# A vision tower's first performer: the loop over images in a new order

## The chip, the cores and the metric

One core of one Trainium2 chip runs the whole program. The metric is the device time of one execution in microseconds (us). The kernel before took 2234.66 us, the median of three runs (2223.88 to 2236.14).

## The reference, cut to what matters

The program computes a tower of five parts on 32 images of 3x128x128. The change lies in the first part alone, the first performer, which the reference writes as follows (`t` is 1024 patches of 147 numbers per image; EMB is 64, M is 32):

```python
t = _unfold(x, 7, 4, 2)                      # 32 images, 1024 tokens, 147 numbers
h = _ln(x, n1g, n1b)
k, q, v = split(h @ kqvw + kqvb)             # 64 each
kp, qp = _prm_exp(k, wrand), _prm_exp(q, wrand)   # exp(x @ w.T - |x|^2/2), 32 features
D = einsum('btm,bm->bt', qp, sum(kp, 1))
kptv = einsum('btd,btm->bdm', v, kp)
y = einsum('btm,bdm->btd', qp, kptv) / D
y = v + (y @ projw + projb)
y + (gelu(_ln(y) @ w1 + b1) @ w2 + b2)
```

After it come a second performer, a projection, two attentions, a mixture of experts, a state-space layer and a gated mixture of experts. They are not touched.

## The kernel before, in words

`patches` works image by image. An image is eight tiles of 128 tokens. The patches are read from a row-ordered copy of the image into one of two buffers `X`; a layer norm's mean is folded into the weights, so only the inverse root is multiplied in.

Every engine runs its own function `body(t, p)`, one call per step `t`; `schedule` writes the first steps out, then a hardware loop of two steps, then the last steps. Nothing plans the order: it is the order of the lines in each `body`, and semaphores hold the engines together. One step moves up to five images along:

- SyncE: copies image t+1 into row order, loads image t, stores image t-4.
- VectorE: `exponent` (squared norms and z) of the second half of image t-2, `finish` of t-4 (the last sum, L1159), `attend` of t-3 (denominators, their reciprocal, y, v added at L1141, statistics of y), `aggregate2`, `statistics` and `aggregate` of image t (L1108, L1112), `normalise2` (L1153), `exponent` of the first half of t-1, `keep_kp` (L1128), a copy of the projected keys and values.
- GpSimd: the inverse roots (L1078 adds epsilon, L1080 is the power), the scaled patches `R` (L1091) and `H` (L1093), and `yb` = y + b2 (L1098).
- ScalarE: copies out of PSUM, squares (L1208), exponentials and Gelu. Exp and Gelu each load a table first.
- TensorE (L1300 to L1355): transposes of image t-1 (`turn_tail` L1246, `turn_main` L1258), the product with the weights, first the 21 remaining rows in slots of 32 rows (`matmul_tails`, L1272), then the 126 main ones (`matmuls`, L1283); keys times values of t-2 (L1312), the turned queries (L1318), the projection KP (L1326), the turned y of t-3 (L1334), first layer (L1343), numerators (L1296), second layer (L1354).

The product with the weights is cut in pieces of 4, 2, 1 and 1 tiles, with the other products set between them. The numerators are eight products, each of 32 rows by 65 columns, in two groups of four with `matmuls` between them; `KPs` holds the same keys and values four times over the partitions, and each product takes one slot of 32 rows of it.

The second performer, in `performer`, already takes its numerators in another way: `BD` holds KP in four copies side by side, a mask leaves of each copy only its own slot of rows (L507), and one product of 128 rows by 260 columns (L732) gives four tiles.

Of the kernel before, what the change touches and what calls it, by code (L numbers as in the profile page):

```python
# [13 lines left out]
PARTS = 128  # L14
# [731 lines left out]
def patches(nc, name, image, rows_c, dst, w):  # L746
# [11 lines left out]
    with ExitStack() as ctx:  # L758
# [13 lines left out]
        names = ("x_in0", "x_in1", "out0", "out1", "border", "stat", "aggr", "eps1", "rstd1", "norm", "trans", "tback", "rem", "kq", "sq", "v", "xd", "z", "exp",  # L772
                 "kv", "kvs", "qt", "rq", "kp", "kps", "num", "den", "rden", "ymul", "y", "yb", "stat2", "aggr2",
                 "eps2", "rstd2", "norm2", "yt", "yts", "m1", "gelu", "m2", "fin", "ones", "zero", "tail", "load", "gate", "edge", "tails", "copied0", "copied1")
# [208 lines left out]
        KPs = st.sbuf("KPs", [PARTS, EMB + 1])  # L983
# [23 lines left out]
        def every_other(t, b):  # L1007

            return t.rearrange("p (c b) e -> p b c e", b=2)[:, b]

# [11 lines left out]
        def schedule(eng, body, end=steps):  # L1022

            for t in range(6):
                body(t, t % 2)
            with eng.Fori(6, end, 2) as t:
                body(t, 0)
                body(t + 1, 1)
            for t in range(end, steps + 4):
                body(t, t % 2)  # L1030

# [3 lines left out]
        def _(sp):  # L1035
# [16 lines left out]
            def body(t, p):  # L1052
                if live(t + 1) and not (isinstance(t, int) and t < EARLY - 1):
                    copy(sp, t + 1, 1 - p)
                if live(t) and not (isinstance(t, int) and t < EARLY):
                    load(sp, t, p)
                if isinstance(t, int) and t == 1:
                    border()
                if live(t - 4):
                    store(t - 4, p)  # L1060

            schedule(sp, body, steps - 2)
# [5 lines left out]
        def _(pool):  # L1068
# [5 lines left out]
            nc.gpsimd.memset(BDz[:], 0.0).then_inc(s["zero"], 1)  # L1074

# [6 lines left out]
            def body(t, p):  # L1082
                l = t - 3
                if live(l):
                    inverse_root(l, "aggr2", "eps2", "rstd2", mv2, rstd2)
                if live(t):
# [3 lines left out]
                    wait(pool, s["trans"], 3 * t)  # L1090
                    nc.gpsimd.tensor_tensor(R[:, :, 1:1 + REM].rearrange("p t (a b) -> p t a b", b=7), windows(p, 18, 3),  # L1091
                                            spread(spread(rstd[:], 2, 3), 3, 7), ALU.mult).then_inc(s["tail"], 1)
                    nc.gpsimd.tensor_tensor(H[:].rearrange("p t (a b) -> p t a b", b=7), windows(p, 0, 18),  # L1093
                                            spread(spread(rstd[:], 2, 18), 3, 7), ALU.mult).then_inc(s["norm"], 1)
                if live(l):
                    pool.wait_ge(s["y"], l + 1)
# [3 lines left out]
            schedule(pool, body)  # L1100

        @block.vector
        def _(dve):
            def statistics(i, p):
                wait(dve, s["eps1"], i)
# [4 lines left out]
            def aggregate(i):  # L1110
                for j in range(tiles):
                    nc.vector.bn_aggr(mv[:, j, :], stats[:, j, :]).then_inc(s["aggr"], 1)  # L1112

            def exponent(i, q):

                tl = slice(4 * q, 4 * q + 4)
                dve.wait_ge(s["sq"], quads * i + q + 1)
                nc.vector.reduce_sum(xd[:, tl, :], sq[:, tl, :, :], axis=AX_X).then_inc(s["xd"], 1)  # L1118
                dve.wait_ge(s["xd"], quads * i + q + 1)
                wait(dve, s["exp"], i)  # L1120
                dve.wait_ge(s["v"], quads * i + q + 1)
                nc.vector.tensor_tensor(z[:, :, tl, :].rearrange("p a t f -> p t a f"), KQ[q][:, :, 3 * EMB:COLS].rearrange("p t (a f) -> p t a f", a=2),
                                        spread(xd[:, tl, :], 3, FEATS), ALU.subtract).then_inc(s["z"], 1)

            def keep_kp(i):
                dve.wait_ge(s["kp"], i + 1)
                wait(dve, s["num"], 2 * i)
                nc.vector.tensor_copy(KPs[:], KP).then_inc(s["kps"], 1)  # L1128

            def attend(i, p):  # L1130
# [6 lines left out]
                wait(dve, s["yb"], i)  # L1137
                for b in range(2):
                    nc.vector.tensor_tensor(every_other(y[:], b), NUM[b][:, :, 0:EMB], spread(rden[:, b, :], 2, EMB), ALU.mult).then_inc(s["ymul"], 1)
# [6 lines left out]
            def aggregate2(i):  # L1146
                for j in range(tiles):
# [14 lines left out]
            def body(t, p):  # L1162
                l = t - 3
                if live(t - 2):
                    exponent(t - 2, quads - 1)
                if live(t - 4):
                    finish(t - 4, p)
                if live(l):
                    attend(l, 1 - p)


                    dve.wait_ge(s["stat2"], tiles * (l + 1))
                    dve.sem_inc(s["gate"], 1)
                    aggregate2(l)
                if live(t):
                    statistics(t, p)
                    dve.wait_ge(s["stat"], tiles * (t + 1))
                    dve.sem_inc(s["gate"], 1)
                    aggregate(t)
                if live(l):  # L1180
                    normalise2(l)
                if live(t - 1):
                    exponent(t - 1, 0)
                if live(t - 2):
                    keep_kp(t - 2)

            schedule(dve, body)

        @block.scalar
        def _(act):  # L1190
            def body(t, p):
                m, k, l = t - 1, t - 2, t - 3
                if live(m):
                    act.wait_ge(s["trans"], 3 * m + 1)
                    nc.scalar.copy(RQ[:, 0:256], bank(3)[:, 0:256]).then_inc(s["rem"], 1)
                    for q in range(quads):
                        act.wait_ge(s["trans"], 3 * m + 2 + q)
                        nc.scalar.copy(hT[0:MAIN, q, :], ps[0:MAIN, q * BANK:(q + 1) * BANK]).then_inc(s["tback"], 1)
                if live(k):
                    act.wait_ge(s["z"], quads * (k + 1))  # L1200
                    wait(act, s["qt"], k)
                    nc.scalar.activation(kpq[:].rearrange("p a t f -> p (a t f)"), z[:].rearrange("p a t f -> p (a t f)"), ACT.Exp).then_inc(s["exp"], 1)

                def squares(q):
                    tl = slice(4 * q, 4 * q + 4)
                    act.wait_ge(s["kq"], quads * m + q + 1)
                    wait(act, s["xd"], quads * m)
                    nc.scalar.activation(sq[:, tl, :, :].rearrange("p t a e -> p t (a e)"), KQ[q][:, :, 0:2 * EMB], ACT.Square,  # L1208
                                         scale=0.5 ** 0.5).then_inc(s["sq"], 1)

                    wait(act, s["y"], m - 1)
                    if isinstance(m, int) and m == 0:
                        act.wait_ge(s["ones"], 3)
                    nc.scalar.copy(v1[1 - p][:, tl, 0:EMB], KQ[q][:, :, 2 * EMB:3 * EMB]).then_inc(s["v"], 1)

                if live(m):
                    squares(0)
                if live(k):
                    act.wait_ge(s["kv"], k + 1)
                    nc.scalar.copy(kvT[:], spread(KV, 1, 4)).then_inc(s["kvs"], 1)  # L1220
                if live(k):
                    act.wait_ge(s["qt"], k + 1)
                    nc.scalar.copy(RQ[:, 256:256 + PARTS * quads], bank(7)[:, 256:256 + PARTS * quads]).then_inc(s["rq"], 1)
                if live(l):
                    act.wait_ge(s["yt"], l + 1)
                    nc.scalar.copy(yT[:].rearrange("p t c -> p (t c)"), bank(7, half)).then_inc(s["yts"], 1)
                if live(l):
                    act.wait_ge(s["m1"], l + 1)
# [1723 lines left out]
```

## Time and profile before

| | |
|---|---|
| Median of the runs | 2234.66 us (2223.88 to 2236.14) |
| Profiled execution | 2229.52 us, span 2227.8 us |
| TensorE busy | 1716.7 us, 77% |
| VectorE, ScalarE, GpSimd busy | 1092.0, 751.6, 734.2 us |
| Mean granted TensorE clock | 0.875 of 2.4 GHz |
| The first performer's loop | from about 31.4 us to about 530 us of the span |

Busy times are sums over one profiled execution. A matmul's end is modelled, and the next may begin before it; therefore the times of TensorE are best read from start to start. An fp32 product stands in the trace as two records or more.

### The profile page before, as it was taken

To read this page: it belongs to the slowest core of one execution; us is meant where nothing else is said; L and a number is where in the kernel's file an instruction comes from. 1 tells how busy PE (TensorE), PEld (TensorE's weight loads), DVE (VectorE), ACT (ScalarE), POOL (GpSimd) and SP (SyncE) were. 2 spreads that over 40 slices of the span, in tenths; PEclk is the share of its full clock that TensorE was granted. 3 is DMA by queue.
4 is the path that set the end of the run, shared out by engine and by line. 5 is a ranking of instruction groups with operands and counts; after the bars stand their busy time and mean duration, and the time that the engine had idled before them with its cause. 6 is when DMAs were issued, how large, how long until landed. Compare 5 with 4: busy or idle time off the path is not lost. (4 is left out here: it accounts for less than half of the span.)

```text
span 2227.8 us, 35707 instructions
## 1 busy us (share of the span) xinstructions
PE 1716.7 (77%) x11543; PEld 1310.8 (59%) x11544; DVE 1092.0 (49%) x3245; ACT 751.6 (34%) x1396; POOL 734.2 (33%) x664
## 2 busy tenths in 40 slices
PE   4898888983799956497768777999639767746897
PEld 3666666651688846376637676999627523335565
DVE  3666566562577631427653753122170179962232
ACT  1555555550255521125213623211114623213110
POOL 2545555441122210043141310333220069940232
PEclk9999999995899978698877966999859989976899
DMA  3222232211333313200000044555230176636111
GB/s 67 53 51 59 55 59 56 53 36 36 97 83 91 89 27 85 60 1 2 12 1 1 2 124 124 163 154 155 76 69 1 31 183 160 159 76 169 41 48 30
DMA packets 219403, 157.95 MB, mean 71 GB/s; under 512 B 116583, under 2 KB 196404, under 8 KB 218794
## 3 DMA queue, kind: packets, MB, share of 16 engines
q1 hardware_dynamic: 203141, 138.82, 25.6%
q0 software_dynamic: 6528, 14.19, 2.2%
q10 hardware_dynamic: 9638, 3.69, 0.7%
q8 instruction: 57, 0.93, 0.2%
q14 instruction: 39, 0.32, 0.1%
HBM read 106.05 MB, written 32.35 MB: 62 GB/s over the span
## 5 line engine op out<-in xcount | busy, mean ns | idle before, releaser
L2180 POOL TENSOR_TENSOR ssm_scan_prod<-ssm_scan_S,ssm_crep 128x1056 f32<-128x1056 f32 x48 | 159.4, 3321 | 157.9 <-DVE ssm_scan_S L2197 157.9
L677 PE MATMUL a_psum<-a_W,a_hT 128*128 128x256 f32 (+1 forms) x640 | 149.9, 382 | 12.5 <-ACT a_hT L586 12.5
L1283 PE MATMUL a_psum<-a_W,a_hT 126*128 126x256 f32 x512 | 144.8, 406 | 0.0
L677 PEld LDWEIGHTS a_psum<-a_W,a_hT 128*128 128x128 f32 (+1 forms) x640 | 118.5, 191 | 30.6 <-ACT a_hT L586 16.4
L2221 PE MATMUL ssm_scan_psum<-ssm_ST,ssm_EW 112*128 112x512 f32 (+1 forms) x288 | 103.6, 497 | 23.3 <-PEq L1935 20.5
L2735 PE MATMUL moe_tiles_psum<-moe_tiles_XT,moe_tiles_mine 96*128 96x128 f32 x960 | 118.7, 280 | 1.9 <-DMA moe_tiles_mine<-moe_W 1.9
L1118 DVE TENSOR_REDUCE a_xd<-a_sq 128x8 f32<-128x512 f32 x64 | 43.9, 685 | 149.5 <-ACT a_sq L1208 149.5
L2735 PEld LDWEIGHTS moe_tiles_psum<-moe_tiles_XT,moe_tiles_mine 96*128 96x128 f32 x960 | 113.0, 194 | 4.9 <-DMA moe_tiles_mine<-moe_W 2.3
L2197 DVE TENSOR_TENSOR_SCAN ssm_scan_S<-ssm_scan_X,ssm_scan_psum 128x1056 f32<-128x1056 f32 x48 | 112.9, 2353 | 5.1 <-issue 0.9
L1283 PEld LDWEIGHTS a_psum<-a_W,a_hT 126*128 126x128 f32 x512 | 89.2, 194 | 32.1 <-issue 18.9
L1080 POOL TENSOR_TENSOR a_rstd<-a_rstd,a_mhalf 128x8 f32<-128x8 f32 x64 | 105.1, 1642 | 5.0
L2221 PEld LDWEIGHTS ssm_scan_psum<-ssm_ST,ssm_EW 112*128 112x128 f32 x288 | 51.4, 192 | 90.0 <-issue 68.0
L1078 POOL TENSOR_TENSOR a_rstd<-a_mv,a_eps 128x8 f32<-128x8 f32 x64 | 22.9, 358 | 235.0 <-DVE a_mv L1148 209.5
L2782 ACT ACTIVATE moe_tiles_GT<-moe_tiles_psum 128x512 f32<-128x512 f32 x80 | 39.1, 490 | 160.5 <-PE moe_tiles_psum L2735 160.4
L2827 DVE TENSOR_TENSOR moe_tiles_Y<-moe_tiles_psum,moe_B 128x192 f32<-128x192 f32 x40 | 14.3, 357 | 156.8 <-PE moe_tiles_psum L2719 156.8
L2209 ACT ACTIVATE ssm_scan_psum<-ssm_scan_psum 128x1056 f32<-128x1056 f32 x48 | 49.7, 1035 | 120.4 <-PE ssm_scan_psum L2221 120.4
L2762 PE MATMUL glu_tiles_psum<-glu_W,glu_tiles_XT 96*128 x192 | 84.6, 585 | 6.3 <-DVE glu_tiles_XT L2812 6.1
L2719 PE MATMUL moe_tiles_psum<-moe_W,moe_tiles_GT 128*128 x480 | 84.5, 326 | 0.0
L2078 PE MATMUL ssm_mlp_psum<-ssm_mlp_xT,ssm_mlp_W 96*128 96x260 f32 (+3 forms) x352 | 82.0, 393 | 0.6 <-ACT ssm_mlp_xT L1903 0.6
L1208 ACT ACTIVATE a_sq<-a_psum 128x512 f32<-128x512 f32 x64 | 38.2, 597 | 129.7 <-PE a_psum L1283 129.7
L2690 POOL DMA_INDIRECT ys<-moe_tiles_Y,moe_target x40 | 39.5, 987 | 128.6 <-DVE moe_tiles_Y L2827 125.7
L2719 PEld LDWEIGHTS moe_tiles_psum<-moe_W,moe_tiles_GT 128*128 128x128 f32 x480 | 77.1, 190 | 0.0
(633 smaller groups left out, 3986.5 us busy)
## 6 DMA issues: line engine op xcount, KB each, us to landing
ssm_scan_grep<-gains SPq DMA_DIRECT2D x48, 528.0 KB, 4.7
moe_tiles_mine<-moe_W SPq DMA_DIRECT2D x40, 576.0 KB, 3.9
a_X<-t SPq DMA_DIRECT2D x168, 96.0 KB
moe_route_raw<-in_L_ffn_w SPq DMA_DIRECT2D x16, 576.0 KB
t<-a_O SPq DMA_DIRECT2D x128, 64.0 KB
xrows<-in_x SPq DMA_DIRECT2D x30, 192.0 KB
a_X<-xrows SPq DMA_DIRECT2D x60, 91.9 KB
proj_X<-t SPq DMA_DIRECT2D x96, 48.0 KB
```

The lines of the kernel that those rows point to most:

```text
L677: last = nc.tensor.matmul(out, hT[0:rows, kt, cols], W[0:rows, kt, :], start=(kt == 0), stop=(kt == nkt - 1))
L1080: nc.gpsimd.tensor_tensor(out[:], out[:], mhalf[:], ALU.pow).then_inc(s[done], 1)
L1118: nc.vector.reduce_sum(xd[:, tl, :], sq[:, tl, :, :], axis=AX_X).then_inc(s["xd"], 1)
L1283: last = nc.tensor.matmul(KQ[q][:, j, :], hT[0:MAIN, q, PARTS * j:PARTS * j + PARTS], W[0:MAIN, :], start=False, stop=True)
L2078: last = nc.tensor.matmul(ps[0:rows_, (n % 4) * BANK:(n % 4) * BANK + GROUP], W1[0:k, kb, c0:c0 + rows_], xT[0:k, kb, GROUP * g:GROUP * g ...
L2180: nc.gpsimd.tensor_tensor(prod[n % 2][:], S[n % 2][:], crep[:, cols], ALU.mult).then_inc(s_prod, 1)
L2197: nc.vector.tensor_tensor_scan(S[n % 2][:], X[n % 2][:], E[n % 2], 0.0, ALU.add, ALU.mult).then_inc(s_scan, 1)
L2209: nc.scalar.activation(E[n % 2], E[n % 2], ACT.Exp).then_inc(s_coef, 1)
L2221: last = nc.tensor.matmul(E[n % 2][:, a:b], EW[:, j, :], ST[:, j // (NCH // 2), HCOLS * h + a:HCOLS * h + b], start=True, stop=True)
L2719: last = nc.tensor.matmul(made(p), GT[p][0:w_, f, :], W2[0:w_, f, bass.ds(e, 1), :].rearrange("p a c -> p (a c)"), start=(f == 0), stop=(f ...
L2735: last = nc.tensor.matmul(hidT(1 - p, f, 1), mine[q][0:HALF + kb, kb, PARTS * f:PARTS * f + PARTS], XT[1 - p][0:HALF + kb, kb, :], start=( ...
L2762: last = nc.tensor.matmul(hid(c), XT[p][0:k, kb, :], W1[0:k, kb, bass.ds(e, 1), cut * c:cut * c + cut].rearrange("p a c -> p (a c)"), star ...
```

## The change

The mathematics stays. What changes in the first performer's loop:

- VectorE's order is now: finish image t-6; block diagonal of t-4; aggregate t-1; exponent second half of t-3; attend and aggregate2 of t-4; statistics of t; normalise2 of t-4; exponent first half of t-2. The aggregation of an image's statistics is a step later than the statistics.
- GpSimd does the first inverse root, R and H ahead of the second inverse root and yb (of t-3).
- ScalarE, TensorE and SyncE get the orders shown below; up to seven images are under way, and the store is of image t-7. The loops of `schedule` have a lag of their own per engine and more steps written out.
- The eight numerators become two products of 128 rows by 260 columns. `KPs` becomes `BD`, made with a mask by one VectorE operation. The halves of y are now contiguous. The mask is built at the start on GpSimd, behind the zeroing of the border (L1074), and VectorE's first operation waits for it.
- Several counters are split by half (kq0, kq1 and so on), and waits are added where buffers are reused across steps.

```diff
+            dve.wait_ge(s["ones"], 7)
...
-                nc.vector.tensor_copy(KPs[:], KP).then_inc(s["kps"], 1)
+                nc.vector.tensor_tensor(BD[:], spread(KP, 1, 4), spread(mask[:], 2, EMB + 1), ALU.mult).then_inc(s["kps"], 1)
...
@@ vector, body
+                if live(t - 6):
+                    finish(t - 6, p)
                 if live(t - 4):
+                    keep_kp(t - 4)
+                if live(t - 1):
+                    aggregate(t - 1)
+                if live(t - 3):
+                    exponent(t - 3, 1)
+                if live(t - 4):
+                    attend(t - 4, p)
+                    aggregate2(t - 4)
                 if live(t):
                     statistics(t, p)
+                if live(t - 4):
+                    normalise2(t - 4)
                 if live(t - 2):
+                    exponent(t - 2, 0)
...
@@ scalar, body (m, k, l, n = t - 1, t - 2, t - 3, t - 4)
+  gelu(n); values(m, 0); squares(m, 0); kvT(k); RQ queries(k); squares(m, 1); values(m, 1);
+  yT(l); hT halves 0, 1 of image t; RQ remainder of t; exp(m)
...
@@ tensor
+            def numerators(i):
+                pe.wait_ge(s["kps"], i + 1)
+                pe.wait_ge(s["rq"], i + 1)
+                wait(pe, s["yts"], i)
+                for q in range(quads):
+                    nc.tensor.matmul(NUM[q].rearrange("p t c -> p (t c)"), RQ[:, 256 + PARTS * q:256 + PARTS * q + PARTS], BD[:].rearrange("p r c -> p (r c)"),
+                                     start=True, stop=True).then_inc(s["num"], 1)
...
             def body(t, p):
+                if live(t - 5):
+                    mlp2(t - 5)
+                if live(t - 4):
+                    turn_y(t - 4)
+                if live(t - 3):
+                    project_keys(t - 3)
+                if live(t - 1):
+                    turn_tail(t - 1)
+                    turn_main(t - 1, 1)
+                if live(t - 3):
+                    numerators(t - 3)
+                if live(t - 4):
+                    mlp1(t - 4)
+                if live(t - 1):
+                    first_half(t - 1)
+                if live(t - 2):
+                    keys_values(t - 2, p)
+                if live(t - 1):
+                    second_half(t - 1)
+                if live(t):
+                    turn_main(t, 0)
+                if live(t - 2):
+                    turn_queries(t - 2)
+                if live(t - 1):
+                    last_mains(t - 1)
```

The two lines under "scalar, body" stand for the new order of that engine's operations, whose own code is unchanged but for its waits. `first_half` and `second_half` hold four remainder products each, and the eight main ones are cut 4, 2 and 2; `mlp1`, `mlp2`, `turn_y`, `project_keys`, `keys_values` and `turn_queries` are the products of before under names of their own.

## Rows read from the trace of the kernel before

**Rows 1.** Page, part 1: busy time, share, instructions.

```profile
PE 1716.7 (77%) x11543; PEld 1310.8 (59%) x11544; DVE 1092.0 (49%) x3245; ACT 751.6 (34%) x1396; POOL 734.2 (33%) x664
```

**Rows 2.** Windows, first to 29th finish, then the drain: length, busy, granted clock, DMA.

```profile
72.45:483.64 411.19, 364.64 (x2578) 251.38 (x2577) 264.54 (x1262) 228.40 (x392) 213.92 (x196) 0.95 0.28 55
483.64:529.99 46.35, 26.86 (x156) 17.59 (x154) 21.02 (x80) 14.52 (x23) 9.23 (x9) 0.69 0.07 18
```

**Rows 3.** Timeline of TensorE, one step: start, duration, line, operation, records, idle before.

```profile
263.64 0.38 PE L1246 MATMUL a_psum<-a_ident,a_R 128*128 128x128 f32 x2
...
269.82 1.13 PE L1283 MATMUL a_psum<-a_W,a_hT 126*128 126x256 f32 x4
272.06 0.44 PE L1326 MATMUL a_psum<-a_projw,a_kvT 65*128 65x65 f32 x2 [1.10 <-ACT a_kvT L1220]
...
272.88 0.60 PE L1283 MATMUL a_psum<-a_W,a_hT 126*128 126x256 f32 x2
273.80 1.12 PE L1343 MATMUL a_psum<-a_yT,a_w 128*128 128x512 f32 x2 [0.32 <-ACT a_yT L1226]
274.86 0.66 PE L1296 MATMUL a_psum<-a_KPs,a_RQ 32*128 32x65 f32 x8
275.44 0.70 PE L1283 MATMUL a_psum<-a_W,a_hT 126*128 126x256 f32 x2
276.07 0.66 PE L1296 MATMUL a_psum<-a_KPs,a_RQ 32*128 32x65 f32 x8
276.67 1.16 PE L1354 MATMUL a_psum<-a_w,a_G 128*128 128x128 f32 x8
277.66 0.38 PE L1246 MATMUL a_psum<-a_ident,a_R 128*128 128x128 f32 x2
278.72 0.55 PE L1258 MATMUL a_psum<-a_ident,a_H 128*126 128x128 f32 x3 [0.24 <-DVE a_O L1159]
```

**Rows 4.** Timeline of TensorE in the second performer: its block-diagonal numerators.

```profile
684.53 0.60 PE L732 MATMUL a_psum<-a_BD,a_RQ 128*128 128x260 f32 x2
684.97 0.61 PE L739 MATMUL a_psum<-a_w,a_G 128*128 128x128 f32 x4
```

**Rows 5.** Windows: a stretch with the clock down, and the second performer.

```profile
139.00:140.00 1.00, 1.00 (x2) 0.00 (x0) 0.00 (x0) 0.88 (x1) 1.00 (x1) 0.55 0.09 12
149.00:150.00 1.00, 1.00 (x4) 0.92 (x5) 0.84 (x10) 0.99 (x2) 0.00 (x0) 0.83 0.27 66
660.00:720.00 60.00, 56.74 (x344) 50.17 (x345) 43.08 (x157) 32.27 (x59) 17.49 (x28) 1.00 0.33 90
```

**Rows 6.** Timeline of VectorE: two finishes, one step apart, and the wait between.

```profile
249.75 0.69 DVE L1159 TENSOR_TENSOR a_O<-a_psum,a_yb 128x512 f32<-128x512 f32 x1
...
254.19 1.76 DVE L1108 BATCH_NORM_STATS2 a_stats<-a_X 128x6 f32<-128x147 f32 x8
...
262.79 0.69 DVE L1118 TENSOR_REDUCE a_xd<-a_sq 128x8 f32<-128x512 f32 x1 [3.91 <-ACT a_sq L1208]
...
263.85 0.68 DVE L1159 TENSOR_TENSOR a_O<-a_psum,a_yb 128x512 f32<-128x512 f32 x1
```

**Rows 7.** Timelines of GpSimd and VectorE where they meet.

```profile
256.83 0.56 POOL L1078 TENSOR_TENSOR a_rstd<-a_mv,a_eps 128x8 f32<-128x8 f32 x1 [0.55 <-DVE a_mv L1112]
...
259.69 1.95 POOL L1093 TENSOR_TENSOR a_H<-a_X,a_rstd 128x1008 f32<-128x1008 f32 x1
...
490.12 1.26 POOL L1098 TENSOR_TENSOR a_yb<-a_y,a_b 128x512 f32<-128x512 f32 x1
490.19 1.75 DVE L1153 TENSOR_TENSOR a_yn<-a_y,a_rstd 128x512 f32<-128x512 f32 x1 [2.04 <-POOL a_rstd L1080]
```

**Rows 8.** Timelines at the loop's start, and an affine select of later.

```profile
31.43 1.80 DVE L1108 BATCH_NORM_STATS2 a_stats<-a_X 128x6 f32<-128x147 f32 x8 [0.32 <-PEq L798]
...
31.88 1.85 POOL L1074 MEMSET a_BDz<- 32x2112 f32 x1
...
534.85 0.29 POOL L60 TENSOR_SCALAR_AFFINE_SELECT a_ident<-a_ident 128x128 f32<-128x128 f32 x1 [0.16 <-POOL a_ident L58]
```

More of the change, by code:

```diff
@@ L1020, in live, with schedule, upto @@
             return 0 <= i < steps if isinstance(i, int) else True
[L1022 to L1024 removed]
+        def schedule(eng, body, lag, end=steps):
+            first = lag + 2 + lag % 2
+            for t in range(first):
                 body(t, t % 2)
[L1026 removed]
+            with eng.Fori(first, end, 2) as t:
                 body(t, 0)
                 body(t + 1, 1)
[L1029 removed]
+            for t in range(end, steps + lag):
                 body(t, t % 2)
+        def upto(n):
+            return min(n, steps) if isinstance(n, int) else n
         block = ctx.enter_context(nc.Block())
@@ L1182, in body @@
-                if live(t - 1):
-                    exponent(t - 1, 0)
+                if live(t - 4):
+                    normalise2(t - 4)
                 if live(t - 2):
-                    keep_kp(t - 2)
-            schedule(dve, body)
+                    exponent(t - 2, 0)
+            schedule(dve, body, 6)
         @block.scalar
         def _(act):
-            def body(t, p):
-                m, k, l = t - 1, t - 2, t - 3
-                if live(m):
[L1194 to L1217, printed above, removed]
@@ new lines, in squares, with values @@
+            def squares(i, q):
+                tl = slice(4 * q, 4 * q + 4)
+                act.wait_ge(s["kq%d" % q], i + 1)
+                wait(act, s["xd%d" % q], i)
+                nc.scalar.activation(sq[:, tl, :, :].rearrange("p t a e -> p t (a e)"), KQ[q][:, :, 0:2 * EMB], ACT.Square,
+                                     scale=0.5 ** 0.5).then_inc(s["sq%d" % q], 1)
+            def values(i, q, p):
+                tl = slice(4 * q, 4 * q + 4)
+                act.wait_ge(s["kq%d" % q], i + 1)
+                wait(act, s["y"], i - 1)
+                if isinstance(i, int) and i == 0:
+                    act.wait_ge(s["ones"], 3)
+                nc.scalar.copy(v1[p][:, tl, 0:EMB], KQ[q][:, :, 2 * EMB:3 * EMB]).then_inc(s["v%d" % q], 1)
@@ L1218, in body @@
+            def body(t, p):
+                m, k, l, n = t - 1, t - 2, t - 3, t - 4
+                if live(n):
+                    act.wait_ge(s["m1"], n + 1)
+                    wait(act, s["m2"], n)
+                    nc.scalar.activation(G[:].rearrange("p t c -> p (t c)"), bank(0, half), ACT.Gelu, bias=b1[:, 0:1]).then_inc(s["gelu"], 1)
+                if live(m):
+                    values(m, 0, 1 - p)
+                    squares(m, 0)
                 if live(k):
                     act.wait_ge(s["kv"], k + 1)
+                    wait(act, s["kp"], k)
@@ new lines, in turn_y, with mlp1 @@
+            def turn_y(i):
+                pe.wait_ge(s["norm2"], i + 1)
+                pe.wait_ge(s["rq"], upto(i + 2))
+                for j in range(tiles // 2):
+                    last = nc.tensor.transpose(bank(7)[:, PARTS * j:PARTS * j + PARTS],
+                                               yn[:, 2 * j:2 * j + 2, :].rearrange("p t e -> p (t e)"), ident[:])
+                last.then_inc(s["yt"], 1)
+            def mlp1(i):
+                pe.wait_ge(s["yts"], i + 1)
+                pe.wait_ge(s["th0"], upto(i + 4))
+                if isinstance(i, int):
+                    wait(pe, s["gelu"], i)
+                nc.tensor.matmul(bank(0, half), w1[:], yT[:].rearrange("p t c -> p (t c)"), start=True, stop=True).then_inc(s["m1"], 1)
```

245 lines of the change are left out of this document (107 added, 138 removed), and 3 rows, old and new, of the table names.

## The prediction

> **What bounds the kernel now.** I read the page's busy times first [rows 1]: TensorE is busy 77% of the span, but that is a mean over five parts with different limits, so the loop has to be read alone. The windows do that [rows 2]: between the first and the 29th finish lie 411.19 us, 28 steps, 14.69 us each, and in them TensorE is busy 364.6 (89%), VectorE 264.5, ScalarE 228.4, GpSimd 213.9. Per step that is 9.45 us of VectorE, 8.16 of ScalarE, 7.64 of GpSimd: TensorE is the nearest to its limit, the others have 4.6 us or more to spare. VectorE even stands still 3.91 us in the middle of a step, until the squares that wait for the last main product [rows 6].
>
> Then one step of TensorE, from start to start [rows 3]: turn_tail begins at 263.64 and 277.66, 14.02 us apart (finish to finish 14.10 [rows 6]). In it TensorE waits for others: from the end of the second cut's two main products (269.82 + 1.13 = 270.95) to KP at 272.06, 1.11 us for ScalarE's copy kvT; before the first layer 0.32 us for yT; 0.24 us for the finish in a part of the steps. A following group that doesn't wait begins some 0.1 to 0.15 before the modelled end of the one ahead (277.66 against 276.67 + 1.16 = 277.83), so a wait costs that more than its idle time.
>
> Last the clock. 28 steps of 14.10 make 394.8; the window is 16.4 longer. The granted clock of the window is 0.95 [rows 2]: about 41 us of it lie at half clock (1.2 instead of 2.4 GHz). One such stretch runs from 139.1 to 149.3 by its two edges [rows 5], 10.2 us, so there are four, at 4.1 us each. The rows don't say what starts a fall; I take TensorE's idle time as the cause.
>
> **The change part by part.** All for one steady step, at full clock.
>
> 1. The waits. kvT of image t-3 is now copied by ScalarE a step ahead of the product that reads it; its cost of 1.11 + 0.13 goes. turn_y comes at the step's start and the first layer some 2.0 us after it, with turn_tail, turn_main and the numerators between; today turn_y and the copy of its result to yT together take less than 1.74 (KP at 272.06, first layer at 273.80), so they fit. 0.32 + 0.1 go. The finish is awaited by turn_main only three images on: 0.24 in one step of two, about 0.2 with its overlap. Exponentials are made half a step ahead of keys times values: some 0.2. Sum 2.0; only the bare idle of the rows is 1.11 + 0.32 + 0.12 = 1.55, the lower bound.
> 2. Numerators. Two groups of four take 275.44 - 274.86 = 0.58 and 276.67 - 276.07 = 0.60 [rows 3]. The product of 128 rows by 260 columns in the second performer takes 684.97 - 684.53 = 0.44 [rows 4]; two make 0.88. Gain 0.3, and from 0.1 (0.15 more for loading the first weights after another kind of product) to 0.35.
> 3. Main products cut 4, 2, 2 instead of 4, 2, 1, 1: the two single ones take 273.48 - 272.88 = 0.60 and 276.07 - 275.44 = 0.63; a pair 1.13 less 0.13 = 1.0. Gain 0.2, from 0 to 0.25.
> 4. VectorE gets 128x260 with a mask for a 128x65 copy. The trace has no product of this kind in this loop, but one of 128x256 from PSUM beside a small operand in z; by 0.42 against 0.22, +0.2 us, off the path as long as VectorE has room. It stands between KP and the numerators, though, with turn_tail and turn_main as cover (0.7 us).
> 5. The start. The mask comes behind the memset of the border (31.88 + 1.85 = 33.73), a memset and two selects of 0.29 each with a handoff of 0.16 [rows 8]: VectorE's first statistics begin at 34.6 instead of 31.43. **+3.2 us**, bounds +2.5 and +4.
> 6. SyncE stores t-7 and no longer waits for a fresh finish in front of the next copy and load. VectorE never waited for a load. Nothing gained; the load still waits for H of t-2 and has about 6 us before the statistics.
>
> 14.02 - 2.0 - 0.3 - 0.2 = 11.5 us per step if TensorE is never idle. By the lower bounds 14.02 - 1.55 - 0.1 = 12.4; by the upper 11.3. I take **11.7**, near the full sum, because the waits are read directly and the rest is small.
>
> **Do the other engines follow at 11.7?** I laid them out from the start of the second layer at 0: it ends at 1.16, finish to 1.8, KP done at 1.9, block diagonal to 2.4 (the numerators begin at 2.5), aggregate to 2.8, exponent to 3.9, attend and aggregate2 to 7.75, statistics to 9.45. GpSimd: aggregate done 2.9, yb of the image before ends 3.2, inverse root 5.3, R and H to 8.2, second inverse root 10.2. VectorE normalises at 10.2, then exponent to 11.9. turn_y wants the first at 12.7 and turn_tail the second at 13.5: about 1.5 us to spare. ScalarE: yT 1.7, hT and remainder to 3.6, z there at 4.0, table and exponentials to 5.9, table and Gelu to 7.8 (needed at 11.7), then it waits for the first main products. The ring through VectorE and GpSimd closes at about 10.6, so TensorE stays the bound, but narrowly.
>
> **Sum.** 28 steps of 11.7 are 327.6 against 411.2: -83.6, of which 16.4 is the clock, which I expect to stay up: the second performer with TensorE busy 56.74 of 60 us has 1.00 [rows 5]. First finish: an image lies 4 steps less 254.19 - 249.75 = 4.4 us, 52.0, between statistics and finish today, and takes 72.45 - 31.43 = 41.0 while the loop fills, 0.79 of it. Now it is 6 steps less about 6.5: 63.7, times 0.79 is 50: **+9** (0 to +12). Drain: from the 29th finish to the end are 46.35 us, two whole rounds through attend, inverse root, Gelu and finish one behind the other, at clock 0.69 [rows 2]. In the new order attend of the last image stands ahead of the finish of the image before, so one round is left: three intervals of about 10, 10 and 8: **-17.7** (-8 to -24). With the start +3.2: -83.6 - 17.7 + 9 + 3.2 = -89.1. From the profiled execution's 2229.5 this gives 2140.4; the median of the runs shown is 5.1 above the profiled time, so I say **2142**.
>
> **A rule that speaks against part 2.** Four products of 32 rows by 65 columns take 0.58 here, where 260 columns at full height take 0.44 [rows 3, 4]. The Trainium skill (TensorE: Matmul & The Clock Gate, Part 3, Measured speedup vs the span model) says that small row tiles run at the same time, the span being that of one product plus some ns per tile; by that alone two rounds of 65 columns would be some 0.22 us (an estimate, twice a quarter of 0.44), and the change would lose 0.66 a step instead of gaining 0.3. The rows don't agree: 1.18 against 0.88 is measured, and decides.
>
> **Rivals.**
> A, VectorE and GpSimd bound. An operation with two SBUF inputs is stopped by GpSimd: yn took 1.75 instead of 0.66 while yb ran, and the epsilon add 0.56 instead of 0.20 beside yn [rows 7]. Today they are set apart. In the new order y + v (two SBUF inputs, at 5.2) falls on R and H (5.3 to 8.2), and yn on yb (10.2). If GpSimd is first both times, VectorE loses 1.95 + 1.1 = 3.05, 1.5 more than there is to spare: 13.3 us a step, 28 x 13.3 = 372.4, in all 2229.5 - 38.8 - 5.5 = **2185**. The Trainium skill (SBUF — State Buffer, Who interferes with whom) has this rule, the whole instruction being blocked, as rows 7 show. Against it: by my layout y + v comes 0.1 ahead of R, so R waits, not it.
> B, the clock still falls. The new order puts turn_y, KP, turn_tail and turn_main in a row, 1.5 us without a wide product. At today's one fall of 10.2 us per 103 us (411.19/4) there are 3.2 in 328 us, each now costing its whole half, 5.1 us: +16, **2158**.
> C, the loop is held as before: ScalarE's order (table load behind its wait, Gelu behind exponentials) or the new reuse waits keep TensorE at 14 us. 28 x 14.1 + 16.4 is what it was, and with 9 + 3.2 - 17.7 the time is **2224**. Against: 3.9 us between Gelu and its use.
> D, slower. The stretch of part B, once every step, keeps the clock down for much of the loop. A share f at half clock makes the step 11.7/(1 - f/2): the loop breaks even with 14.69 at f = 0.41. At f = 0.55, 16.1 us: 28 x 16.1 = 451, +40, with fill and drain about +8: **2277** at worst. Against: in the loop today the same transposes beside idle time bring it down only one step in six.
>
> **Chances.** Forecast 0.60; B 0.17; A 0.12; C 0.06; D 0.05. The measurement tells 0.5% (11 us) from no change: faster 0.89, same 0.06, slower 0.05. With 11.3 per step and the better drain it would be 2122; the range goes from there to A, 2187. C and D are left out, and what is under the forecast's lower end.
>
> **What would show it.** Finish to finish 11.4 to 12.0 us; no idle of TensorE before KP and the first layer; granted clock 1.00 through the loop; L732's kind of record (380 ns) for the numerators; block diagonal about 0.43; first statistics at 34.6; last finish near 440 instead of 530; everything behind it unchanged. y + v above 0.7 or yn at 1.75 speaks for A, clock 0.95 for B, idle TensorE with a steady 14 for C. I am wrong if the step is above 12.4 at full clock.

## The result, and the profile after

The kernel after takes **2116.99 us** (median of four runs, 2113.64 to 2117.62) against 2231.6 for the kernel before in the same runs: ratio 0.950, interval 0.947 to 0.952. I had said 2142, with 2122 to 2187 as the range: the direction and the case (TensorE the bound, full clock) were right, the gain was larger than I said, and the time lies 5 us below the range.

The profiled execution has a span of 2111.6 us against 2227.8. Part 1 of its page, columns as in [rows 1]:

```profile
PE 1653.1 (78%) x11159; PEld 1297.2 (61%) x11160; DVE 1096.1 (52%) x3245; ACT 744.2 (35%) x1394; POOL 732.7 (35%) x667
```

TensorE is busy for 64 us less. VectorE, ScalarE and GpSimd are busy as long as before (1096, 744 and 733 us), in a shorter span. The windows that answer to [rows 2] do, first to 29th finish and 29th finish to the end of the loop:

```profile
84.86:389.53 304.67, 302.13 (x2238) 237.55 (x2237) 264.89 (x1237) 222.78 (x392) 206.94 (x192) 1.00 0.34 70
389.53:417.10 27.57, 18.32 (x72) 12.03 (x70) 13.01 (x55) 7.50 (x12) 7.49 (x7) 0.62 0.11 29
```

TensorE is busy 302.1 of 304.7 us (it was 364.6 of 411.2), at a granted clock of 1.00. The parts, against the forecast:

| | before | after | change | forecast |
|---|---|---|---|---|
| first finish | 72.45 | 84.86 | +12.4 | +12.2 (+3.2 start, +9 fill) |
| 28 steps | 411.19 | 304.67 | -106.5 | -83.6 |
| drain | 46.35 | 27.57 | -18.8 | -17.7 |
| span behind the loop | | | -3.3 | 0 |
| sum | | | -116.2 | -89.1 |

First finish and drain came out within 1.1 us. The code behind the loop is the same in both kernels; no row here shows a cause for its -3.3 us, and the profiled execution after is itself 3.35 us below the median of its runs, so I take it as scatter. Of the miss of 27.1 us, 22.9 are in the step: 10.88 us on the mean (10.85 and 10.96 in turn) where I took 11.7.

One step of TensorE after, from one second-layer product to just ahead of the next (279.94), and below the second dots one row of the next step; columns as in [rows 3]:

```profile
269.10 1.06 PE L1358 MATMUL a_psum<-a_w,a_G 128*128 128x128 f32 x8
269.99 0.60 PE L1341 MATMUL a_psum<-a_ident,a_yn 128*128 128x128 f32 x4
270.43 0.33 PE L1327 MATMUL a_psum<-a_projw,a_kvT 65*128 65x65 f32 x2
270.60 0.39 PE L1268 MATMUL a_psum<-a_ident,a_R 128*128 128x128 f32 x2
271.03 0.63 PE L1279 MATMUL a_psum<-a_ident,a_H 128*126 128x128 f32 x4
271.49 1.04 PE L1334 MATMUL a_psum<-a_BD,a_RQ 128*128 128x260 f32 x4
272.37 1.02 PE L1350 MATMUL a_psum<-a_yT,a_w 128*128 128x512 f32 x2
273.32 0.71 PE L1284 MATMUL a_psum<-a_Wrem,a_RQ 32*128 32x256 f32 x8
...
277.45 1.13 PE L1290 MATMUL a_psum<-a_W,a_hT 126*128 126x256 f32 x4
278.42 0.60 PE L1279 MATMUL a_psum<-a_ident,a_H 128*126 128x128 f32 x4
278.86 0.38 PE L1321 MATMUL a_psum<-a_ident,a_kpq 128*128 128x128 f32 x2
279.08 1.03 PE L1290 MATMUL a_psum<-a_W,a_hT 126*128 126x256 f32 x4
...
281.99 0.63 PE L1279 MATMUL a_psum<-a_ident,a_H 128*126 128x128 f32 x4 [0.15 <-DVE a_O L1179]
```

In this step no record shows idle time ahead of it. Only turn_tail (270.60) to turn_main (271.03) is 0.43 instead of 0.22, since turn_main waits for the finish; in every other step that wait shows as 0.15 us of idle time (281.99). Read from start to start as in the prediction, this is where the step's 3.2 us went:

| stretch, start to start | before | after | less |
|---|---|---|---|
| two main products, wait for kvT | 2.24 | 0.97 | 1.27 |
| third and fourth main product, wait for yT | 1.55 | 0.86 | 0.69 |
| numerators | 1.18 | 0.88 | 0.30 |
| turn_tail and both halves of turn_main, wait for the finish | 1.54 | 1.33 | 0.21 |
| KP and turn_y | 0.82 | 0.61 | 0.21 |
| turned queries | 0.35 | 0.22 | 0.13 |
| first layer | 1.06 | 0.95 | 0.11 |
| second layer | 0.99 | 0.89 | 0.10 |
| four main products (with a wait), keys times values, remainders | 4.29 | 4.13 | 0.16 |

The four rows ahead of the last one are products that the change only moved. I had given them nothing.

VectorE in the same step:

```profile
268.00 0.69 DVE L1173 TENSOR_TENSOR a_yn<-a_y,a_rstd 128x512 f32<-128x512 f32 x1 [0.50 <-POOL a_rstd L1089]
...
270.19 0.69 DVE L1179 TENSOR_TENSOR a_O<-a_psum,a_yb 128x512 f32<-128x512 f32 x1 [0.37 <-PE a_psum L1358]
270.80 0.43 DVE L1144 TENSOR_TENSOR a_BD<-a_psum,a_mask 128x260 f32<-128x260 f32 x1
...
271.69 0.65 DVE L1134 TENSOR_REDUCE a_xd<-a_sq 128x8 f32<-128x512 f32 x1
...
274.00 0.69 DVE L1158 TENSOR_TENSOR a_y<-a_y,a_v 128x512 f32<-128x512 f32 x1
```

and GpSimd:

```profile
274.26 0.77 POOL L1098 TENSOR_TENSOR a_R<-a_X,a_rstd 128x168 f32<-128x168 f32 x1
```

The block diagonal takes 0.43. y + v at 274.00 comes 0.26 ahead of R at 274.26, takes its plain 0.69, and R is stretched from 0.48 to 0.77; yn takes 0.69, not the 1.75 of [rows 7] (once, while the loop fills, at 71.69, it took 1.74). VectorE stands still 0.50 and 0.37 us in the two waits shown.

At the start the mask costs what was said:

```profile
34.61 1.80 DVE L1121 BATCH_NORM_STATS2 a_stats<-a_X 128x6 f32<-128x147 f32 x8 [3.22 <-POOL a_mask L1082]
...
46.73 1.38 DVE L1121 BATCH_NORM_STATS2 a_stats<-a_X 128x6 f32<-128x147 f32 x6 [6.88 <-DMA a_X<-xrows]
```

The second line is one that I did not foresee: the third image's load lands only at 46.7, and VectorE waits 6.88 us for it. (The row is cut at the end of its window; the wait ahead of it is whole.)

### The profile page after: what moved, and what is told of

Read it like the earlier page. It is cut to its first block and busy times, and to the rows that moved or that the text cites. A ratio compares the mean times of both kernels' runs of the same rounds, so it can differ in the third digit from the quotient of the medians.

```text
span 2111.6 us, 35070 instructions
## 1 busy us (share of the span) xinstructions
PE 1653.1 (78%) x11159; PEld 1297.2 (61%) x11160; DVE 1096.1 (52%) x3245; ACT 744.2 (35%) x1394; POOL 732.7 (35%) x667
## 5 line engine op out<-in xcount | busy, mean ns | idle before, releaser
L677 PEld LDWEIGHTS a_psum<-a_W,a_hT 128*128 128x128 f32 (+1 forms) x640 | 118.5, 191 | 30.7 <-ACT a_hT L586 16.4
L1290 PE MATMUL a_psum<-a_W,a_hT 126*128 126x256 f32 x512 | 134.7, 396 | 0.0
L2109 PEld LDWEIGHTS ssm_mlp_psum<-ssm_mlp_xT,ssm_mlp_W 96*128 96x128 f32 (+3 forms) x352 | 66.7, 190 | 14.3 <-ACT ssm_mlp_xT L1934 0.9
L1109 POOL TENSOR_TENSOR a_yb<-a_y,a_b 128x512 f32<-128x512 f32 x32 | 40.7, 1272 | 93.0 <-DVE a_O L1179 93.0
L2265 PE MATMUL ssm_scan_psum<-ssm_scan_prod,ssm_SEL 128*32 128x264 f32 x384 | 32.3, 409 | 45.5 <-POOL ssm_scan_prod L2211 45.5
```

Source lines behind the costliest of these rows:

```text
L677: last = nc.tensor.matmul(out, hT[0:rows, kt, cols], W[0:rows, kt, :], start=(kt == 0), stop=(kt == nkt - 1))
L1290: last = nc.tensor.matmul(KQ[q][:, j, :], hT[0:MAIN, q, PARTS * j:PARTS * j + PARTS], W[0:MAIN, :], start=False, stop=True)
L2109: last = nc.tensor.matmul(ps[0:rows_, (n % 4) * BANK:(n % 4) * BANK + GROUP], W1[0:k, kb, c0:c0 + rows_], xT[0:k, kb, GROUP * g:GROUP * g ...
```

## The experiments

The question was where the missing 0.8 us a step comes from, whether idle time was the cause of the clock's falls, and how near the other engines are. Theory L, formed from the table above: a group of products whose first weight load cannot run ahead of the stream, because it stands behind a wait or beside products of 32 rows, costs about 0.1 us more, and in a dense stream that goes. Its rival O: a group costs what its own records say, only the idle time in the rows is to be had. "Step" is finish to finish, mean of 28 in one profiled execution. The diffs are shortened, and some of their lines are in words.

**1. The new numerators alone, in the old order.**

```diff
 kernel before
-                nc.vector.tensor_copy(KPs[:], KP).then_inc(s["kps"], 1)
+                nc.vector.tensor_tensor(BD[:], spread(KP, 1, 4), spread(mask[:], 2, EMB + 1), ALU.mult)...
-                for j in (0, 1, 4, 5) if first else (2, 3, 6, 7): ...32-row products
+                one 128 x 260 product for each half
```

> The kernel before in its old order with the numerators as two block-diagonal products (and the mask at the start, +3 us). Theory O: 0.44 for each in place of 0.58 and 0.60, the step falls by 0.3 to 13.7 us, 2231 - 8 + 3 = 2226. Theory L: the groups behind the 32-row ones (main product, second layer) also get their weight loads covered, the step falls by 0.5 to 13.5, 2231 - 14 + 3 = 2220. The clock's falls stay under both.

Measured: 2207.39 us (2201.32 to 2210.32), ratio 0.989 (0.986 to 0.992); step 13.78. TensorE's timeline of it:

```profile
264.38 1.12 PE L1349 MATMUL a_psum<-a_yT,a_w 128*128 128x512 f32 x2 [0.32 <-ACT a_yT L1236]
265.33 0.60 PE L1303 MATMUL a_psum<-a_BD,a_RQ 128*128 128x260 f32 x2
265.77 0.60 PE L1293 MATMUL a_psum<-a_W,a_hT 126*128 126x256 f32 x2
266.21 0.60 PE L1303 MATMUL a_psum<-a_BD,a_RQ 128*128 128x260 f32 x2
266.65 1.05 PE L1360 MATMUL a_psum<-a_w,a_G 128*128 128x128 f32 x8
267.54 0.38 PE L1256 MATMUL a_psum<-a_ident,a_R 128*128 128x128 f32 x2
...
268.83 0.66 PE L1268 MATMUL a_psum<-a_ident,a_H 128*126 128x128 f32 x4 [0.48 <-DVE a_O L1169]
```

From the first layer to turn_tail it is 3.16 us, against 277.66 - 273.80 = 3.86 in [rows 3]: 0.70 less, and only 0.30 of it is the numerators' own. The first layer went from 1.06 to 0.95, the second from 0.99 to 0.89, and the single main product between the numerators from 0.63 to 0.44. So the part of L that speaks of 32-row products holds for these. The part on waits does not hold for the first layer, which stands right behind a wait of 0.32 and takes 0.95 all the same. The experiment also takes the reason from part 3 of my prediction: a single main product among full-height ones costs 0.44, half of the pair's 0.86 to 0.87. Cutting costs nothing; the 32-row neighbours did. The step fell by less than 0.70, from 14.10 to 13.74 outside one fall of the clock, and the wait for the finish grew from 0.24 to 0.48. The time is 13 us under the lower expectation mainly because I had left the falls in: one step of 15.18 is all that is left of them.

**2. The kernel after with the old numerators.** The same edit, undone in the new order: the two groups of four stand one behind the other, and the second waits for the first.

> The changed kernel in its new order with the eight old numerators of 32 rows, the second four behind a wait for the first four. Theory O: step 10.88 + 0.3 = 11.2 us, and the start is 3 us earlier without the mask: 2117 + 9 - 3 = 2123. Theory L: the first layer behind them loses its early weight load too and the second group of four stands exposed: 11.4 to 11.5, 2117 + 16 - 3 = 2130.

2140.74 us (2130.64 to 2143.2), ratio 0.959; step 11.52, +0.64. Its timeline:

```profile
264.09 1.39 PE L1332 MATMUL a_psum<-a_KPs,a_RQ 32*128 32x65 f32 x16
265.41 1.12 PE L1349 MATMUL a_psum<-a_yT,a_w 128*128 128x512 f32 x2
266.47 0.71 PE L1278 MATMUL a_psum<-a_Wrem,a_RQ 32*128 32x256 f32 x8
```

The numerators take 1.32 (1.18 before, with another product between the groups) and the first layer behind them is back at 1.06: 0.55 of 0.64. The rest stands ahead of them, at turn_main, 0.56 instead of 0.46. The part of the 1.32 that is the wait of the second group is not separated. The clock stayed at 1.00 in the 28 steps. 28 steps at 0.64 are 18 of the 24 us between the two times, both above what I had expected. The first finish, at 89.58, is 4.7 later, though the statistics begin 3.1 earlier: while the loop filled, one y + v took 2.10 beside GpSimd, TensorE stood still 2.65 us (until 73.06), and its clock was 0.88, 0.50 and 0.60 in the three stretches of 5 us from 70 to 85 us.

**3. The wait for kvT alone, in the old order.** ScalarE copies kvT and the queries ahead of the first squares.

```diff
 kernel before, scalar body
-                if live(m):
-                    squares(0)
                 if live(k): ...copy kvT, copy RQ queries
+                if live(m):
+                    squares(0)
```

> The kernel before with one swap: ScalarE copies kvT and the turned queries ahead of the squares and values of the first half. It takes away TensorE's wait before KP (1.11 us of idle time a step) and nothing else; the waits for yT and the finish stay. Theory O (own times: a wait costs its idle time and the 0.13 us by which groups otherwise overlap, what I used in the prediction): the step falls from 14.02 to 12.8 us; KP keeps its 0.36 us to the next group's start. Theory L (a group behind a wait also pays for its first weight load, which in a dense stream runs ahead): KP falls to about 0.17, the step to 12.6. On the clock: if the idle time before KP starts the falls, they vanish and 28 steps save another 16 us: 2231 - 39 - 16 = 2176 (L) or 2181 (O); if they stay, 2192 to 2197.

2189.47 us (2186.63 to 2190.93), ratio 0.981 (0.979 to 0.984); step 13.28 and no fall of the clock in the loop. TensorE:

```profile
263.64 1.13 PE L1283 MATMUL a_psum<-a_W,a_hT 126*128 126x256 f32 x4
264.61 0.33 PE L1326 MATMUL a_psum<-a_projw,a_kvT 65*128 65x65 f32 x2
265.22 0.66 PE L1334 MATMUL a_psum<-a_ident,a_yn 128*128 128x128 f32 x4 [0.28 <-DVE a_yn L1153]
```

The wait of 1.11 is gone and the two main products take 0.97, as in the kernel after; KP's record is 0.33 instead of 0.44. But the step gave only 0.8 of 1.27, less than either theory said: a new wait of 0.28 for yn stands behind KP. A wait read from a row is worth its length only if no other engine's ring (a chain of work that closes on itself once a step) is as long.

**4. Both small edits in the old order.**

> The kernel before with both small edits: kvT copied ahead of the squares, and the numerators as two block-diagonal products. Apart they took the step from 14.10 to 13.30 and 13.74 us. If TensorE's order alone held the loop, the two would add up to 14.10 - 1.43 - 0.70 = 12.0 us (theory L's full price of each). Theory R, that the old order closes a ring (squares of the second half, exponent, finish, second half of turn_main), says that a part comes back as a longer wait for the finish, as in e_bd_only (0.48 us in place of 0.24): 12.8 us, 2231 - 36 - 16 + 3 = 2182.

2196.52 us (2191.57 to 2201.4), ratio 0.985; step 13.28, the same as with experiment 3 alone, where I had expected 12.8. (The time is longer than there because the first finish, behind the mask, is 5.1 later.) What the numerators save on TensorE comes back whole, in TensorE's wait for the finish, 0.26 in experiment 3:

```profile
276.53 0.66 PE L1268 MATMUL a_psum<-a_ident,a_H 128*126 128x128 f32 x4 [0.94 <-DVE a_O L1169]
```

and VectorE in the same stretch:

```profile
274.27 0.69 DVE L1128 TENSOR_REDUCE a_xd<-a_sq 128x8 f32<-128x512 f32 x1 [2.37 <-ACT a_sq L1218]
...
275.79 0.69 DVE L1169 TENSOR_TENSOR a_O<-a_psum,a_yb 128x512 f32<-128x512 f32 x1 [0.37 <-POOL a_yb L1106]
```

VectorE waits 2.37 us for the squares of the last main product, then makes the exponent, and only then the finish, for which the next image's turn_main waits. Last main product, squares, exponent, finish, turn_main: that ring of the old order closes at about 13.3 us in both experiments, though TensorE has some 0.7 less to do in the second. The new order opens it: VectorE's finish (270.19 in the kernel after) stands ahead of the exponent of the second half (271.69) instead of behind it. That this, more than any single wait, is what the new order is worth follows from the rows; no run changes VectorE's order alone.

**5. Idle time put back into the new order.** KP waits for ScalarE's first copy of hT.

```diff
 kernel after, tensor body
                 if live(t - 3):
+                    if live(t - 1):
+                        pe.wait_ge(s["th0"], t)
                     project_keys(t - 3)
```

> The changed kernel with one wait added: KP waits for ScalarE's first hT copy, which by the trace ends 1.28 us after KP's start, so TensorE stands still 1.3 us a step. Theory O: step 10.88 + 1.28 + 0.13 = 12.3 us, KP at 0.17 us to the next start. Theory L: KP goes back to 0.36 and the step to 12.5. Clock: if an idle stretch beside transposes starts the falls, the granted clock of the loop drops below 1.00 again, some four falls at 4 us each; if not, it stays 1.00. O without falls 2117 + 39 = 2156, L with falls 2117 + 45 + 16 = 2178.

2155.72 us (2152.7 to 2161.55), ratio 0.968; step 12.19, +1.31.

```profile
270.29 0.60 PE L1341 MATMUL a_psum<-a_ident,a_yn 128*128 128x128 f32 x4
272.06 0.44 PE L1327 MATMUL a_psum<-a_projw,a_kvT 65*128 65x65 f32 x2 [1.16 <-ACT a_hT L1247]
272.33 0.39 PE L1268 MATMUL a_psum<-a_ident,a_R 128*128 128x128 f32 x2
```

A bare idle of 1.16 costs 1.31 in all. In its own place it costs 1.33 (turn_y to KP is 1.77 instead of 0.44), KP is 0.27 instead of 0.17 to the next start and the numerators are 0.98 instead of 0.88; on the other side turn_tail is down from 0.43 to 0.23, since the finish is now there in time. And the clock stayed at 1.00 in all 28 steps, with as much idle time ahead of KP as the kernel before had (1.10), though without the waits for yT and the finish (0.32 and 0.24). This much idle time alone does not start the falls.

**6. Both put back: idle time and 32-row numerators in the new order.**

> The kernel after with both of two earlier edits: KP waits for the first copy of hT (about 1.16 us of idle TensorE a step) and the numerators are again eight products of 32 rows by 65 columns. Neither alone brought a clock fall. Theory both: idle time and the 32-row numerators together start the falls of the kernel before, so some steps of the 28 are 2 us or more longer and the granted clock of the loop is 0.95 to 0.98. Rival, order: the falls belong to the old order of the products, the clock stays at 1.00 and the step is the sum of the two edits, 10.88 + 1.31 + 0.64 = 12.8.

2194.30 us in one run; clock 0.92 in the loop, and eleven of the 28 steps are 14.2 to 16.0 us where the others take 12.55 to 12.8. So the falls came back, in the new order, with the two together. Here one begins:

```profile
127.80 0.43 PE L1321 MATMUL a_psum<-a_projw,a_kvT 65*128 65x65 f32 x2 [1.16 <-ACT a_hT L1241]
128.08 0.39 PE L1262 MATMUL a_psum<-a_ident,a_R 128*128 128x128 f32 x2
128.30 0.60 PE L1273 MATMUL a_psum<-a_ident,a_H 128*126 128x128 f32 x4
128.83 1.39 PE L1332 MATMUL a_psum<-a_KPs,a_RQ 32*128 32x65 f32 x16
130.15 1.84 PE L1349 MATMUL a_psum<-a_yT,a_w 128*128 128x512 f32 x2
```

Windows of it, columns as in [rows 2], before and after that point:

```profile
128.00:130.00 2.00, 1.93 (x24) 1.62 (x23) 1.66 (x11) 0.86 (x2) 1.01 (x3) 1.00 0.09 26
130.00:132.00 2.00, 2.00 (x10) 0.46 (x8) 1.84 (x7) 1.72 (x2) 1.92 (x3) 0.61 0.22 65
```

The clock goes from full (2.4 GHz) to half (1.2 GHz) inside the second window, whose mean is 0.61, behind idle time, transposes and 32-row numerators in a row; the first layer's record grows from 1.12 to 1.84. That stretch is what precedes the fall, but it is not the whole condition: the step before has the same stretch (KP at 115.13, behind 1.16 of idle time) and the clock stays at 1.00 there.

**7. VectorE's room: 8 more bn_stats a step.**

```diff
 kernel after, vector body, ahead of normalise2(t - 4)
+                    for j in range(tiles):
+                        nc.vector.bn_stats(junk[:, j, :], y[:, j, :])
```

> The changed kernel with eight more statistics of y per step on VectorE (1.11 us), written to a tile that nobody reads, between the statistics and normalise2. It measures how narrowly TensorE is the bound. VectorE stands idle 0.41 + 0.50 us a step. If VectorE has only that to spare, the step grows by about 0.2 us, to 11.1 (2123). If the added work meets the ring through GpSimd in full (rival A's mechanism), it grows by 0.6 or more, to 11.5 (2134). If TensorE has more room ahead than I think, nothing changes: 10.9.

2117.11 us (2115.47 to 2121.83), ratio 0.949; step 10.93, +0.05 for 1.1 us of work, less than the 0.2 that VectorE's waits would have made. TensorE stays the bound.

**8. The same with 24, 3.1 us.**

> The kernel after with 24 more bn_stats of 64 columns per step on VectorE, ahead of normalise2 (about 3.3 us; 8 of them, 1.1 us, made the step 0.05 longer). This is the loss of VectorE that rival A of the prediction supposed. Theory: VectorE becomes the bound and the ring through it has about 1.1 us to spare, so the step is 10.9 + 3.3 - 1.1 = 13.1 or a little more. Rival: VectorE has more room than its idle time shows, as its waits move too, and the step stays under 12.

2210.75 us in one run, loop clock 0.95. The undisturbed steps are 12.76 and 13.08, mean 12.9, so VectorE's ring has about 3.1 - 2.0 = 1.1 us to spare (I had expected 13.1). The other eleven take 15.2 to 15.6. TensorE in such a one:

```profile
275.84 0.66 PE L1345 MATMUL a_psum<-a_ident,a_yn 128*128 128x128 f32 x4 [1.03 <-DVE a_yn L1174]
...
276.99 0.41 PE L1272 MATMUL a_psum<-a_ident,a_R 128*128 128x128 f32 x2 [0.32 <-DVE a_z L1139]
277.92 0.91 PE L1283 MATMUL a_psum<-a_ident,a_H 128*126 128x128 f32 x4 [0.52 <-DVE a_O L1180]
278.62 1.94 PE L1338 MATMUL a_psum<-a_BD,a_RQ 128*128 128x260 f32 x4
```

GpSimd and then VectorE behind it:

```profile
281.58 1.95 POOL L1103 TENSOR_TENSOR a_H<-a_X,a_rstd 128x1008 f32<-128x1008 f32 x1
```

```profile
281.89 2.18 DVE L1159 TENSOR_TENSOR a_y<-a_y,a_v 128x512 f32<-128x512 f32 x1
```

1.87 us of idle time in three pieces, among transposes, and the numerators run at half clock: 1.94 instead of 1.04. So y + v comes behind R and H instead of ahead of them (0.31 behind H's start) and takes 2.18 instead of 0.69. Rival A's mechanism is real, and here it came by way of rival B's. The numerators are full-height ones, so 32-row numerators are not needed for a fall where there is more idle time than the 1.16 of experiment 5.

**9. A shorter path for the finish: second layer half a step earlier.** `mlp2(t - 4)` between turn_queries and last_mains instead of `mlp2(t - 5)` at the step's start.

> The changed kernel with the second layer of an image moved from the head of TensorE's step to the step before, between the turned queries and the last two main products. Its finish can then come 0.87 us earlier and turn_main's second half no longer waits for it. If TensorE's order is the bound (my theory): the step falls by that wait, 0.2 us, to 10.68, the time by 5.6 to 2111. If instead the ring through VectorE and GpSimd closes at the same length (rival), the wait only moves, to the block diagonal or turn_y, and the step stays at 10.9.

2128.64 us (2121.7 to 2130.49), ratio 0.953; step 11.11 (10.83 and 11.40 in turn), 0.2 longer, where I expected 10.68. The wait for the finish went, and another came:

```profile
264.75 1.12 PE L1334 MATMUL a_psum<-a_BD,a_RQ 128*128 128x260 f32 x4 [0.19 <-ACT a_yT L1242]
```

with ScalarE ahead of it:

```profile
263.26 0.60 ACT L1209 ACTIVATE a_sq<-a_psum 128x512 f32<-128x512 f32 x1 [1.06 <-PE a_psum L1290]
...
264.00 0.61 ACT L1242 COPY a_yT<-a_psum 128x512 f32<-128x512 f32 x1
```

The last main products end 0.9 later, their squares stand in ScalarE's queue ahead of the copy yT, and y + v now starts 0.04 behind R (267.20 and 267.16) and takes 0.98 instead of 0.69 in this step. The expectation fell because I moved a product without moving what ScalarE does behind its neighbour.

**10, 11. The mask ahead of the border's zeroing,** first on top of experiment 9, then on the kernel after alone.

```diff
 kernel after, GpSimd's start
-            nc.gpsimd.memset(BDz[:], 0.0).then_inc(s["zero"], 1)
             memset and two selects of mask
+            nc.gpsimd.memset(BDz[:], 0.0).then_inc(s["zero"], 1)
```

> The same as e_m2_early, and the mask is built before the border's memset, so that VectorE's first statistics need not wait for it. They begin at about 32.9 instead of 34.61 us: another 1.8 us, 2109 if the start is on the path; 2111 if the fill is held by the load of the third image, which the statistics wait for at 46.7 us in the changed kernel.

2126.17 us (2119.39 to 2127.21): first finish 2.55 earlier than in experiment 9, step still 11.11; I had expected 2109 to 2111.

> The kernel after, with the mask of the block diagonal built on GpSimd ahead of the zeroing of the border instead of behind it; nothing else. In the run that moved the mask and the second layer together the first finish came 2.55 us earlier. Theory: the start alone moves, first finish near 82.4 instead of 84.9, steps as in the kernel after (10.88), time 2.5 us less, about 2114.5. Rival: the third image's load sets the fill anyway (6.9 us wait at 46.7), the first finish stays within 1 us and the time at 2117.

2116.86 us (2112.36 to 2118.72, five runs), ratio 0.948 (0.946 to 0.950). The first finish is at 82.76 instead of 84.86, the last at 414.26 instead of 416.31, so the loop does end 2.05 earlier; in the time of the program, whose runs scatter by 4 to 6 us, that does not show (expected: 2114.5). A version that beats the kernel after measurably was not found.

## Why the prediction was right where it was, and wrong in size

- **The bound and the waits (part 1): right.** TensorE bounds the loop, the waits for kvT and yT are gone; the one for the finish became shorter. Forecast 2.0; the table has 1.27 for kvT, 0.42 for yT (0.32 + 0.1 of the 0.69) and 0.21 at turn_main, 1.9 together, and 0.16 in the stretch that had a wait ahead of keys times values.
- **Numerators (part 2): right** as to their own place, 0.30. The bounds held. The rule of the Trainium skill that was weighed there (TensorE: Matmul & The Clock Gate, Part 3, Measured speedup vs the span model) lost again: two groups of four small row tiles, the second waiting for the first, took 1.32 (experiment 2), longer than two full-height products by 0.44, not shorter.
- **Cut of the main products (part 3): size near, reason wrong.** 0.27 against 0.2, but a cut costs nothing by itself (experiment 1). Of the two lengths that I compared with the pair, the 0.60 is the length of a record and no distance to a next start.
- **The step that failed: everything else on TensorE, which the sum for the step (14.02 - 2.0 - 0.3 - 0.2) held constant without a reason.** KP with turn_y, turned queries, first and second layer lost 0.55 us a step together, 15.4 us in 28 steps. Part 2 of my prediction had the effect in its hands ("0.15 more for loading the first weights after another kind of product") and used it only against the gain. The Trainium skill has a possible mechanism (TensorE: Matmul & The Clock Gate, Architectural detail: the array is 16× 32×32, not 1× 128×128): the engine's queue can pull weight loads ahead of products in flight. It would fit that KP behind a wait takes 0.27 instead of 0.17 (experiment 5) and the first layer beside 32-row numerators 1.06 instead of 0.95 (experiments 1 and 2); it leaves open why a wait of 0.32 ahead of the first layer cost nothing more in experiment 1, and why the first layer beside the remainders, also of 32 rows, takes 0.95 in the kernel after. That the numerators' form costs their neighbours is shown; whether it is the load, or the change between 32-row and full-height products itself, or something else at these places, no run isolates.
- **The margin: wrong way.** From the sum of 11.5 I went up to 11.7. The layout of the other engines gave 10.6 for their ring, VectorE could take some 1.1 us more work at the step of 10.88 (experiment 8), and 0.2 for caution was not in any row. 0.2 x 28 is 5.6 of the 22.9 us. Without it the forecast would have been 2136, still high.
- **The last line of the sum.** 2140.4 and 5.1 are 2145.5, not the 2142 that I wrote; the slip went the lucky way by 3.5 us.
- **The clock: effect right, cause half right.** It stayed up (1.00), and the 16.4 us came. But not only because idle time of 1.1 us went: in the steady steps it stays up with that alone (experiment 5) and with the 32-row numerators alone (2); with both it falls (6, one run). In the old order, removing either removed nearly all falls: none in experiment 3, one small one in experiment 1.
- **Start and drain: right; fill: luck.** 34.61 against 34.6, and -18.8 against -17.7. The first finish, 84.86 against 84.65, is two errors that cancel: in steady steps an image now lies 6 x 10.88 less 6.39 (276.58 - 270.19), 58.9 us, between statistics and finish, not 63.7, and it took 50.25 of them while the loop filled, 0.85, not 0.79. With the right step and the factor of 0.79 I would have said 46.5 and been 3.7 us early.
- **The range.** Its low end stood on 11.3 per step, called a sum of the upper bounds; those that I had written down give 14.02 - 2.0 - 0.35 - 0.25 = 11.4. A term left out of the list has no bound.

**Rivals.** A (2185): not the case in the steady steps; R waits for y + v, as laid out. B (2158), C (2224), D (2277): not the case; clock 1.00, step 10.88.

## What to carry to other kernels

When waits on a nearly full engine go and the form of some products changes, the products beside them can get cheaper too (0.55 of 14 us here): price the whole step by rows of the same products in a dense stretch, not the old groups less their idle time. A wait in a row is worth its length only up to the next ring through the other engines (13.3 us here), so follow the ring before trusting the sum. Where a forecast stands on a sum, ask what happens to the items that the change only moves.

## What the runs showed of the hardware

- A full-height group was some 0.1 us shorter when no 32-row numerators stood next to it: first layer 1.06 to 0.95, second 0.99 to 0.89, a single main product 0.63 to 0.44 (two such neighbours). Behind a wait KP took 0.27 instead of 0.17 and the numerators 0.96 (experiment 9) instead of 0.88, but the first layer 0.95 in experiment 1 as without one.
- Eight products of 32 rows by 65 columns take 1.18 or 1.32 in two groups of four, two of 128 rows by 260 columns 0.88.
- When VectorE's y + v and GpSimd's R and H overlap, the one that starts first keeps nearly its own length: y + v 0.69 and R 0.77 instead of 0.48 when y + v starts 0.26 ahead, y + v 2.18 when H starts 0.31 ahead of it.
- In the steady steps of the new order 1.16 us of idle time or 32-row numerators alone brought no fall of the clock, both together did, and so did 1.87 us of idle time among transposes without 32-row numerators (one run each). Why a fall comes only in some of the steps that look alike, here and in the kernel before, stays open.
